# GpSimd injects units 0, 2, 4, 6, 8, 10, 15, 20, 26 and adds step sizes in units 0, 2, 6; the step input has two buffers

## What is computed

```python
u = silu(conv4(x @ W_u) + conv_b)                  # 1024 channels
dt, B, C = split(u @ W_xproj)                      # 32, 16, 16 columns
delta = softplus(dt @ W_dt + b_dt)
def step(h, ins):                                  # over time
    dA = jnp.exp(d_t[..., None] * A)
    h = dA * h + (d_t * u_t)[..., None] * B_t[:, None, :]
    y_t = jnp.einsum('bds,bs->bd', h, C_t)
y = (y + u * Dp) * silu(z);  out = y @ W_out
```

## Time and profile before

| | us |
|---|---|
| median of 3 runs | 3949.91 (3949.03 to 3950.27) |
| the profiled execution | 3946.52 |
| its span in the trace | 3944.4 |
| VectorE busy | 3646.4, 92% of the span |
| GpSimd busy | 3451.7, 88% |
| TensorE busy (matmul) | 3506.4, 89% |
| ScalarE busy | 2830.4, 72% |

### The profile page before, as it was taken

How to read it: one execution, slowest core, us unless ns; L and a number is a source line. 1 busy time by engine, 2 the same in 40 slices (tenths; PEclk the granted TensorE clock), 3 DMA queues, 4 the chain that set the end, 5 groups by cost and what they waited for, 6 DMA issues and landing times. The chain is left out here.

```text
span 3944.4 us, 43314 instructions
## 1 busy us (share of the span) xinstructions
PE 3506.4 (89%) x10938; PEld 1931.7 (49%) x10938; DVE 3646.4 (92%) x3133; ACT 2830.4 (72%) x6002; POOL 3451.7 (88%) x1860
## 2 busy tenths in 40 slices
PE   6789899999899999899989899989899899899887
PEld 3545455545455444455444455444455444445443
DVE  0499999999999999999999999999999999999998
ACT  1477777777777877777877777877777777677775
POOL 0298889998889998889998889998889998889999
PEclk9899999999999999999999999999999999999999
DMA  2111101111101111101111101111100111100110
GB/s 106 50 53 56 55 9 50 53 55 55 55 8 50 52 55 55 55 14 45 53 55 55 55 16 42 52 55 55 55 21 37 53 55 55 55 26 28 49 49 8
DMA packets 50715, 183.77 MB, mean 47 GB/s; under 512 B 7340, under 2 KB 33204, under 8 KB 42068
## 3 DMA queue, kind: packets, MB, share of 16 engines
q1 hardware_dynamic: 48880, 174.17, 11.5%
q10 hardware_dynamic: 1636, 7.83, 0.5%
HBM read 164.15 MB, written 17.83 MB: 46 GB/s over the span
## 5 line engine op out<-in xcount | busy, mean ns | idle before, releaser
L407 POOL TENSOR_TENSOR st<-st,bc 128x1024 f32<-128x1024 f32 x1024 | 2399.2, 2360 | 310.6 <-DVE st L843 310.5
L843 DVE TENSOR_TENSOR_SCAN st<-dec,st 128x1024 f32<-128x1024 f32 x1024 | 2310.0, 2277 | 26.6 <-ACT dec L460 20.3
L668 PE MATMUL y_ps<-st,ident 128*128 128x512 f32 x4096 | 1984.9, 613 | 309.7 <-POOL st L407 308.3
L460 ACT ACTIVATE dec<-delta,decay 128x254 f32<-128x254 f32 x4096 | 1696.8, 467 | 623.6 <-DVE st L843 608.3
L668 PEld LDWEIGHTS y_ps<-st,ident 128*128 128x128 f32 x4096 | 745.1, 192 | 1178.9 <-issue 582.2
L831 DVE TENSOR_TENSOR st<-du,bc 128x1024 f32<-128x1024 f32 x736 | 884.6, 1202 | 4.0 <-ACT du L446 4.0
L398 POOL TENSOR_TENSOR st<-du_sb,bc 128x1024 f32<-128x1024 f32 x288 | 679.5, 2360 | 0.1
L869 DVE SCALAR_TENSOR_TENSOR u<-d_ps,chan,u 128x250 f32<-128x250 f32 (+2 forms) x768 | 308.7, 472 | 68.1 <-ACT u L500 68.0
L706 PE MATMUL d_ps<-xnT,wxz 128*128 128x256 f32 x1024 | 250.5, 388 | 55.5 <-DVE u L869 55.5
L706 PEld LDWEIGHTS d_ps<-xnT,wxz 128*128 128x128 f32 x1024 | 191.0, 191 | 157.0 <-DVE u L869 107.1
L718 PE MATMUL d_ps<-xnT,wxz 128*128 128x256 f32 x1024 | 247.3, 385 | 13.6 <-ACT zs L509 13.5
(11 more groups left out here) (98 smaller groups left out, 2452.4 us busy)
## 6 DMA issues: line engine op xcount, KB each, us to landing
bc<-bc_dram SPq DMA_DIRECT2D x64, 2048.0 KB, 9.5
xg<-x_dram SPq DMA_DIRECT2D x32, 256.0 KB, 11.4
x_dram<-xg SPq DMA_DIRECT2D x32, 256.0 KB, 2.0
last_x<-x_dram SPq DMA_DIRECT2D x32, 256.0 KB, 2.6
out_dram<-last_x SPq DMA_DIRECT2D x32, 256.0 KB, 2.2
bc<-w_inT_dram ACTq DMA_DIRECT2D x1, 4096.0 KB
adjt<-adjT_dram SPq DMA_DIRECT2D x32, 128.0 KB, 11.1
bc<-w_out_dram ACTq DMA_DIRECT2D x1, 2048.0 KB
```

What stands on the lines that cost most here:

```text
L407: nc.gpsimd.tensor_tensor(st[:, sl, :, :, :], st[:, sl, :, :, :], bc[:, p, 1, SU * q:SU * q + SU, None, :].to_broadcast([P, SU, 2, T]), AL ...
L460: a = nc.scalar.activation(dec[:, v % 2, s, j, :].rearrange("p (b t) -> p b t", b=PAIR)[:, :, 1:], delta[:, p, 2 * i + j, :].rearrange("p ...
L668: mm = nc.tensor.matmul(y_all, ident[:, :], st[:, sl, s, :, :].rearrange("p j t -> p (j t)"), start=False, stop=(q == Q - 1 and s == SU - ...
L843: nc.vector.tensor_tensor_scan(h, dec[:, v % 2, :, :, :].rearrange("p s j t -> p (s j t)"), h, 0.0, ALU.mult, ALU.add).then_inc(S["scanned ...
```

## The change

Nine units are GpSimd's, before and after, but other ones. Six of them are now in the first third of a group. `delta` for i = 1, 2, 3 is made at v = 0, 2, 6, and `du_sb` at v = 2, 9, 17. Of the next group's units, 0 and now also 2 are injected before the group begins (at v = 29 and 31). `du_sb` has two buffers, so that step_input(i) waits for the copy of i - 2 and not of i - 1.

```diff
-POOL_UNITS = (0, 4, 8, 12, 16, 20, 24, 27, 30)
-POOL_INJECTS = {0: 4, 5: 8, 8: 12, 12: 16, 16: 20, 20: 24, 23: 27, 26: 30}
-POOL_DELTAS = {2: 1, 9: 2, 14: 3}
-POOL_DUS = {4: 1, 11: 2, 18: 3}
-NEXT_DELTA, NEXT_DU, NEXT_INJECT = 27, 28, 29
+POOL_UNITS = (0, 2, 4, 6, 8, 10, 15, 20, 26)
+POOL_INJECTS = {1: 4, 3: 6, 5: 8, 7: 10, 11: 15, 16: 20, 22: 26}
+POOL_DELTAS = {0: 1, 2: 2, 6: 3}
+POOL_DUS = {2: 1, 9: 2, 17: 3}
+NEXT_DELTA, NEXT_DU, NEXT_INJECTS = 27, 28, {29: 0, 31: 2}
...
-        du_sb = sb("du_sb", [P, 2, T])
+        du_sb = sb("du_sb", [P, 2, 2, T])
...
-                        if v == NEXT_INJECT:
-                            inject(pool, k + 1, r, 0)
+                        if v in NEXT_INJECTS:
+                            inject(pool, k + 1, r, NEXT_INJECTS[v])
...
-                wait(pool, "du_copied", JP * g + i)
-                wait(pool, "p_injected", NP * g + pool_before(Q * i))
-                nc.gpsimd.tensor_tensor(du_sb[:, :, :], delta[:, r, 2 * i:2 * i + 2, :],
+                wait(pool, "du_copied", JP * g + i - 1)
+                wait(pool, "p_injected", NP * g + pool_before(Q * (i - 1)) if i else NP * (g - 1) + pool_before(Q * (JP - 1)))
+                nc.gpsimd.tensor_tensor(du_sb[:, i % 2, :, :], delta[:, r, 2 * i:2 * i + 2, :],
```

More of the change, by code:

```diff
@@ L397, in inject @@
                 wait(pool, "summed", U * g + v + 1 - SLOTS)
-                nc.gpsimd.tensor_tensor(st[:, sl, :, :, :], du_sb[:, None, :, :].to_broadcast([P, SU, 2, T]),
+                nc.gpsimd.tensor_tensor(st[:, sl, :, :, :], du_sb[:, i % 2, None, :, :].to_broadcast([P, SU, 2, T]),
                                         bc[:, r, 0, SU * q:SU * q + SU, None, :].to_broadcast([P, SU, 2, T]),
@@ L445, in copy_du @@
                 wait(act, "injected", ND * k + dve_before(Q * i))
-                nc.scalar.activation(du[:, :, :], du_sb[:, :, :], ACT.Copy).then_inc(S["du_copied"], 1)
+                nc.scalar.activation(du[:, :, :], du_sb[:, i % 2, :, :], ACT.Copy).then_inc(S["du_copied"], 1)
             def decays(act, k, p, v):
```

## The result

| | before | after |
|---|---|---|
| median, us | 3949.47 (3947.16 to 3950.27, 4 runs) | 3992.46 (3987.89 to 3994.59, 4 runs) |
| span of the profiled execution | 3944.4 | 3986.1 |
| mean granted clock of TensorE | 0.979 | 0.955 |

The ratio is 1.0108, with an interval of 1.0091 to 1.0126. The forecast was half a per cent less, 3932, in a range of 3908 to 3955: wrong in its sign.

The account below looks back on a forecast made before the run. VectorE, busiest at 113.67 of 118.2 us a group, was taken to bound the kernel. Terms of -0.55 us a group over 29 groups gave -16; with -3.6 and +2.8 at the end, -17: 3932 to 3933 us, range 3908 to 3955.

Parts of the forecast that it names:

- Gate at v=18: VectorE's gate at the 18th unit of a group no longer waits for TensorE's sum of unit 15: minus 1.73 us a group.
- wait at v=1: Convolution taps at v=1 wait less for ScalarE's `u`, down to the 0.49 us of v=3: minus 0.49 a group.
- v=5: Without VectorE's injection of unit 6, ScalarE's chain makes scan(5) and the taps there wait: plus 0.88 us a group.
- Unit 16: VectorE now injects it, right behind scan(14), and waits for ScalarE's new `du` copy: plus 0.45 us a group.
- Scan(27): VectorE's scan of unit 27 waits less for ScalarE's `dec`, from 0.51 to about 0.1: minus 0.4 us a group.
- gate at v=10: VectorE arrives sooner and waits for TensorE's sum of unit 7, 0.9 us in one group of five: plus 0.17 a group.
- Unit 24: VectorE now injects it and waits for ScalarE's `du` copy, behind Abs and Relu: plus 0.57 us a group.
- The last group: Without convolution, early GpSimd injections aren't hidden; gate at v=10 and scan(10) wait for c(7): plus 2.8 us in all.
- the two groups before it: Groups 29 and 30, without graph work: GpSimd's lag no longer holds up VectorE at the next inj(0), 3.6 us off for both.
- Slower: the `du` copy comes as late as it does now: Injections of units 16 and 24 wait 1.37 and 1.70 us, 2.05 above forecast: +64, 3996; above 3958, chance 0.12.
- TensorE takes the saved time: TensorE keeps 0.75 us more wait a group, at v=10 or v=1: +23, about 3955; 3942 to 3958, chance 0.20.
- the last rival: Each of two table loads at v=3 holds ScalarE 1.4 us longer, scan(5) comes 2.8 later: +86, 4018; chance 0.01.

## Why the prediction was wrong

In the mean of the 28 steady groups a group takes 119.21 us, and took 118.12: plus 1.09 where minus 0.55 was forecast, 1.64 off. By the terms of the sum:

- *Gate at v=18 and wait at v=1* (minus 1.73, minus 0.49): right. No wait at the gate in a steady group; c(15) starts 0.11 us after scan(15), 0.3 was the bound; v=1 waits 0.45.
- *v=5* (plus 0.88): right, 0.71 before scan(5) and 0.08 before the taps.
- *Unit 16* (plus 0.45): right, 0.34, and 0.37 in the mean.
- *Scan(27), gate at v=10* (minus 0.4, plus 0.17): no wait at either, a little better.
- *Unit 24* (plus 0.57): **the step that failed.** The mechanism was put rightly, VectorE asking 5.50 us after scan(21)'s start for a copy behind the Abs and Relu behind the dt product. "TensorE's product should be ready about 0.1 after that point" stands there without a row. It held where TensorE had its full clock at that place, as in the second and fourth group, with 0.39. The mean of the 28 groups is 2.68, 2.1 more than forecast, or 59 us; the other terms together came out 0.5 a group better. I had taken TensorE's waiting for GpSimd off as a pure gain, and hadn't asked what TensorE would do with the time: it idles 2.3 us before the gate of v=18, where it used to be held up by GpSimd in small pieces (0.46 and 1.12 us around that gate in the kernel before), and in that place its clock now falls for 6.8 us in 24 groups.
- *The last group* (plus 2.8): the place was right, the size not. In it GpSimd's injections of units 4, 6 and 8 are themselves late and the gate of v=10 after them:

```profile
3879.19 4.69 DVE L843 TENSOR_TENSOR_SCAN st<-dec,st 128x1024 f32<-128x1024 f32 x2 [2.23 <-POOL st L398]
...
3888.54 4.47 DVE L843 TENSOR_TENSOR_SCAN st<-dec,st 128x1024 f32<-128x1024 f32 x2 [3.54 <-POOL st L398]
...
3895.46 4.47 DVE L843 TENSOR_TENSOR_SCAN st<-dec,st 128x1024 f32<-128x1024 f32 x2 [1.34 <-POOL st L398]
...
3905.29 0.69 DVE L850 TENSOR_TENSOR zs<-y_ps,zs 128x512 f32<-128x512 f32 x1 [4.24 <-PE y_ps L668]
```

  The group takes 120.8 us, 7.3 more than before. In the two groups before it I had taken 3.6 off, and they give 1.9. The first scan starts 3.6 us later too (180.4 against 176.8), which I hadn't in the sum and haven't traced; in all the other variants it starts between 179.5 and 185.3, whatever units they have. The first group takes 2.2 more. The 28 steady groups make up 30.5 of the 41.7.
- *The rivals.* "Slower: the `du` copy comes as late as it does now" had the place, and its 3996 is near the 3992 measured, but by luck: it had 1.37 at unit 16 and 1.70 at unit 24, and 0.37 and 2.68 were measured. Its argument against, that the waits hang on GpSimd's lag, was true and did not help: the lag went and the clock took its place. "TensorE takes the saved time" had the cause, the time at 1.2 GHz, but looked for it at v=10 (or a wait left at v=1), not at v=18. Neither put the two together, and I gave them 0.12 and 0.20. I had listed the gate's clock at v=10 as 0.17 us; the same question had to be put for each product in front of the two copies.
- *The table load.* ScalarE's chain at v=3 kept its length, 4.52 us from the first load to `dec`(5) in both kernels (2098.18 to 2102.70 in a late group of the changed one), so the last rival is out.

**What stays open.** The gap before the gate is 2.35 us in a group where the clock stays and 2.33 in one where it falls, so its length alone does not decide. That the groups settle at 119.3 and 119.6, with the slow stretch at the same place each time, is seen and not explained; the experiments show only that every edit made here at these waits moved it or broke it up. So no more than the order of the loss could have been forecast for this choice of units, not its exact size.

## What to carry to other kernels

When you take a helper's lag away, the engine that it held up in small pieces may idle in one piece. For TensorE ask, at every such gap, who waits for the first products after it, and price them at 1.2 GHz as well as at 2.4. When a tile is handed from one engine to another, look at which unit it is: the first one after a copy or a gate has the least slack, and here it is worth leaving to the engine that needn't wait for the copy. Split a change of several tables into its parts: one of these was worth 1.7%, and the other took 2.8% away.

## What was unexpected in the hardware

- TensorE's clock settles into the loop. In 24 groups in a row the clock was 1.2 GHz at the same place, one where VectorE pays for it, at no change of the work. The same kernel ran its second group in 116.95 us and most of the later ones in 119.5. The Trainium skill ("TensorE: Matmul & The Clock Gate", Part 1) says that the throttled state is the default and that activity releases it; the runs agree: with products repeated in the gap, which are of no use, the stretch behind it was granted 1.00 instead of 0.66, and with both gaps filled the changed kernel was 53 us faster. A kernel that is bound by another engine can be slowed by it, over a chain of TensorE, ScalarE and VectorE.
- Filling one gap moved the slow stretch to another one and left the time about where it was (4002 against 3992); filling both helped.
